# Moving SiLUs, moments and additions between steps, and one product from POOL to VectorE, in a Mamba and mixture-of-experts kernel

## The reference

```python
h = layernorm(layernorm(x)) @ in_proj_w.T            # 256 -> 512 channels
h = silu(sum(pad(h)[k:k + L] * conv_w[:, k] for k in range(4)))
proj = h @ x_proj_w.T                                # dt (1), B (16), C (16)
dt = softplus(proj[0] * dt_proj_w + dt_proj_b)
# for each t, each of 512 channels, each of 16 states n:
state = exp(A[n] * dt[t]) * state + B[t, n] * h[t]
y[t] = sum_n state[n] * C[t, n] + D * h[t]
out = silu(y) @ out_proj_w.T + shortcut
x1 = x + layernorm(out)
# then: x1 + layernorm(shared_swiglu(xn) + routed_swiglu(xn)), 8 experts, the best one per token
```

## Time and profile before

| | |
|---|---|
| median of 3 runs | 1410.12 us |
| the profiled execution | 1411.66 us |
| its span, first to last instruction | 1409.9 us |
| PE busy | 1173.1 us (83%) |
| VectorE busy | 1090.0 us (77%) |
| POOL busy | 1088.5 us (77%) |
| ACT busy | 770.8 us (55%) |
| mean granted TensorE clock | 0.938 of full speed |

### The profile page before, as it was taken

How to read it: one execution, slowest core, us unless ns; L and a number is a source line. 1 busy time by engine, 2 the same in 40 slices (tenths; PEclk the granted TensorE clock), 3 DMA queues, 4 the chain that set the end, 5 groups by cost and what they waited for, 6 DMA issues and landing times.

```text
span 1409.9 us, 15087 instructions
## 1 busy us (share of the span) xinstructions
PE 1173.1 (83%) x4782; PEld 520.5 (37%) x4783; DVE 1090.0 (77%) x1449; ACT 770.8 (55%) x1275; POOL 1088.5 (77%) x565
## 2 busy tenths in 40 slices
PE   5667678786787887888679698788999999999996
PEld 2222223222331422322233242233556655566653
DVE  4598999999999999999998989799241115776675
ACT  5757468676876876867787686556431111111111
POOL 0589999999999999999999999999112824444553
PEclk9898899899999999989998999899999999999998
DMA  3921211240150122124024012300269522222220
GB/s 108 275 67 62 90 60 32 75 150 0 67 189 1 62 99 96 32 75 149 2 74 166 1 62 95 129 0 31 90 237 321 161 75 82 81 81 79 83 66 15
DMA packets 72066, 127.64 MB, mean 91 GB/s; under 512 B 8759, under 2 KB 48448, under 8 KB 67904
## 3 DMA queue, kind: packets, MB, share of 16 engines
q1 hardware_dynamic: 60432, 103.72, 22.2%
q0 software_dynamic: 7152, 16.81, 3.8%
q10 hardware_dynamic: 4416, 6.29, 1.4%
HBM read 97.79 MB, written 31.76 MB: 92 GB/s over the span
## 4 chain that ended last, share of the span: by engine, by line
PE 48%; DVE 21%; ACT 13%; POOL 11%; issue 6%; DMA 0%; DVEq 0%; POOLq 0%; ACTq 0%; SPq 0%
DVE state L1090 12%; PE psX L1647 10%; POOL state L511 6%; PE psX L1582 5%; PE psY L1529 5%; PE bank L1451 4%; PE bank L1486 3%; ACT psX L763 3%; PE psY L1595 3%; POOL bx L500 3%; DVE acc L1025 3%; DVE bx L1078 3%; PE bank L1664 2%; PE psY L1664 2%; POOL lt L516 2%
## 5 line engine op out<-in xcount | busy, mean ns | idle before, releaser
L511 POOL TENSOR_TENSOR state<-state,cbc 128x1024 f32<-128x1024 f32 x256 | 605.8, 2390 | 14.8 <-DVE state L1090 14.7
L1090 DVE TENSOR_TENSOR_SCAN state<-psX,bx 128x1024 f32<-128x1024 f32 x256 | 578.5, 2279 | 31.7 <-ACT psX L763 13.5
L763 ACT ACTIVATE psX<-dt,aneg 128x511 f32<-128x511 f32 x512 | 330.6, 679 | 193.5 <-DVE state L1090 192.8
L500 POOL TENSOR_TENSOR bx<-xh,bbc 128x1024 f32<-128x1024 f32 x120 | 290.3, 2420 | 59.2 <-DMA bbc<-bc_rows 43.3
L1529 PE MATMUL psY<-state,ident 64*64 64x512 f32 x2048 | 284.4, 649 | 18.3 <-POOL state L511 18.3
L1486 PE MATMUL bank<-prow,ident 128*128 128x512 f32 x272 | 170.6, 713 | 114.9 <-DVE bx L1078 114.9
L1078 DVE TENSOR_TENSOR bx<-xh,bank 128x1024 f32<-128x1024 f32 x136 | 162.8, 1197 | 9.3 <-PE bank L1486 9.1
L1529 PEld LDWEIGHTS psY<-state,ident 64*64 64x64 f32 x2048 | 63.9, 139 | 201.7 <-issue 128.8
L961 ACT ACTIVATE sg<-psX 128x512 f32<-128x512 f32 x39 | 23.3, 597 | 196.6 <-PE psX L1647 191.3
L1486 PEld LDWEIGHTS bank<-prow,ident 128*128 128x128 f32 x272 | 48.3, 210 | 205.9 <-DVE bx L1078 169.0
L581 POOL DMA_INDIRECT ysl<-shared_rows,idx x39 | 40.3, 1033 | 80.3 <-DVE idx L1258 75.6
(11 more groups left out here) (200 smaller groups left out, 1726.5 us busy)
## 6 DMA issues: line engine op xcount, KB each, us to landing
cbc<-bc_rows SPq DMA_DIRECT2D x32, 1024.0 KB, 4.7
bbc<-bc_rows SPq DMA_DIRECT2D x16, 1024.0 KB, 6.2
slot_in<-ao SPq DMA_DIRECT2D x1, 5011.5 KB, 35.1
xsl<-slot_in SPq DMA_DIRECT2D x39, 128.5 KB
xin<-in_x SPq DMA_DIRECT2D x8, 512.0 KB, 4.3
xr<-in_x SPq DMA_DIRECT2D x8, 512.0 KB, 5.5
x_rows<-ao SPq DMA_DIRECT2D x8, 512.0 KB, 2.9
xn_rows<-xr SPq DMA_DIRECT2D x8, 512.0 KB, 3.2
```

Of the source, the lines that this page charges most:

```text
L500: nc.gpsimd.tensor_tensor(bx[q % RB][:], xh[par][:, h * CH:(h + 1) * CH], bbc[:, n // 2].unsqueeze(1).broadcast_to([P, CH, L]), ALU.mult). ...
L511: nc.gpsimd.tensor_tensor(w[:], w[:], cbc[:, n].unsqueeze(1).broadcast_to([P, CH, L]), ALU.mult).then_inc(weighted, 1)
L763: e = nc.scalar.activation(decay[q % RD][:, c, 1:L], dt[par][:, h * CH + c, 1:L], ACT.Exp, scale=aneg[:, h * CH + c, n:n + 1])
L1090: nc.vector.tensor_tensor_scan(st[q % RS][:].rearrange("p c t -> p (c t)"), decay[q % RD].rearrange("p c t -> p (c t)"), bx[q % RB][:].rea ...
```

## The change

It does these things:
- step 12 leaves the list of POOL, so VectorE makes 18 products per sequence and POOL 14;
- both SiLUs and the table load behind them are issued at q = 9 instead of 10, so ahead of the decays of step 12;
- the moments of `lead` are computed at q = 24 instead of 29;
- at q = 26 and 27 ACT does the part of `back` ahead of the part of `front`;
- VectorE adds the output projection at q = 17 and 19 instead of 16 and 18, and copies the router's logits at q = 21 instead of 20; TensorE computes those at 20 instead of 19.

```diff
--- before.py
+++ after.py
@@ -37,7 +37,7 @@
     CH = C // H
     Q = H * N
     PN = N // 2
-    BY_POOL = [q % 2 == 0 and q not in (22,) for q in range(Q)]
+    BY_POOL = [q % 2 == 0 and q not in (12, 22) for q in range(Q)]
     PQ = sum(BY_POOL)
     DQ = Q - PQ
     NTH_P = [sum(BY_POOL[:q]) for q in range(Q + 1)]
@@ -633,7 +633,7 @@
                 return last
 
             def lead(f, par, q):
-                if q == 29:
+                if q == 24:
                     act.wait_ge(mv0_ready, f + 1)
                     moments(3, f, mv0[par], 1.0 + EPS, eps2c)
                 if q == 30:
@@ -653,7 +653,7 @@
                     act.wait_ge(inproj_ready, C * f + c + 1)
                     nc.scalar.activation(acc[:, c], psF[:], ACT.Identity,
                                          scale=cw[:, c, TAPS - 1:TAPS]).then_inc(tap_done, 1)
-                if q == 10:
+                if q == 9:
                     act.wait_ge(conv_done, C * (f + 1))
                     if not (isinstance(f, int) and f < 2):
                         act.wait_ge(y_kept, H * (f - 1))
@@ -775,13 +775,15 @@
                         keep_y(i - 1, 1)
                     if do_scan and q == N + SUM_LAG - 1:
                         keep_y(i, 0)
+                    if do_back and q in (26, 27):
+                        back(i - 1, q)
                     if do_front:
                         front(i + 1, 1 - par, q)
-                    if do_back:
+                    if do_back and q not in (26, 27):
                         back(i - 1, q)
                     if not do_front:
                         early(q)
-                    if q == 10 and (do_front or do_back):
+                    if q == 9 and (do_front or do_back):
                         ln_exp_tables()
                     if do_scan and q == 8:
                         act.wait_ge(mv0_ready, i + 1)
...
@@ -1040,13 +1042,13 @@
             def back(b, q):
-                if q in (16, 18):
+                if q in (17, 19):
                     h = q // 2 - 8
...
-                if q == 18:
+                if q == 19:
                     dve.wait_ge(ao_done, 2 * b + 2)
                     stats(1, cb, b, ao, mv[1], mv_ready[1])
...
-                    if do_choose and q == 20:
+                    if do_choose and q == 21:
                         choose(i - 2)
...
@@ -1559,7 +1561,7 @@
-                    if q == 19 and i >= 2:
+                    if q == 20 and i >= 2:
                         choose(i - 2)
```

More of the change, by code:

```diff
@@ L927, in load_group @@
                               xnT_d[LATE_FROM + g]).then_inc(xg_loaded[g % 2], 16)
-            for q in range(10):
+            for q in range(9):
                 back(NB - 1, q)
             keep_y(NB - 1, 1)
-            back(NB - 1, 10)
+            back(NB - 1, 9)
             for c in range(FC):
@@ L1170, in _ @@
             sh_act(0, 0, 1)
-            back(NB - 1, 16)
+            back(NB - 1, 17)
             sh_act(0, 0, 2)
-            back(NB - 1, 18)
+            back(NB - 1, 19)
             sh_act(0, 0, 3)
```

## The result

The changed kernel took 1434.1 us (median; 1431.3 to 1440.1) against 1410.8 for the kernel before on the same chip: ratio 1.0169, interval 1.0154 to 1.0185. Forecast were 1403 and a range that ended at 1415. The profiled execution took 1433.3, its span is 1431.5.

What follows compares the result with a forecast made beforehand. It took a ring of waits through VectorE, ACT and TensorE as the bound, not POOL. Turns 1 to 5 -3.5, turn 6 +0.8, turn 7 +1.1, turn 0 -5.5: -7.1 us, from 1410.12 to 1403.0; range 1390 to 1415.

Steps and rivals of the forecast that it cites:

- Choose moves with 0.12 us: nothing: Router's logits, copied by VectorE a step later: 0.12 us of work changes place, counted as no cost.
- Product 12, the dt projection's delay: On TensorE, spread 13 waits for product 12 and holds the dt projection, which ends at 579.9 against 577.1.
- rival 2: Delayed dt projection runs at half clock on TensorE: +2.6 us in seven turns, +18, giving 1421; chance 0.17.
- The waits that follow: After the dt projection: product 17 starts 1.0 late, scan 17 waits 1.45 more, the addition's 2.18 wait goes.
- the wait of 0.74: VectorE's wait at scan 13, forecast to go because the SiLUs are issued a step sooner.
- The joins: VectorE's two joins wait for a boundary between POOL's instructions: 1.85 and 1.7 us, today 1.35 and 1.77.
- ACT's moves: Moments at step 24, back first in steps 26 and 27: -1.5 us a turn, bounds 0 to -2.5.
- Turn 0: First join starts mid POOL instruction, ends near 144.4 instead of 149.5: -5.1, and -0.4 from the moments, -5.5.
- The end: Turns 6 and 7: +0.8 us without moments to move, +1.1 without a convolution.
- Rival 1: POOL bounds the turn after all, so each turn loses its product, 2.3 us, giving 1391; chance 0.15.
- Rival 3: A join starting in the last 0.2 us before POOL's boundary costs up to 6.9 us: up to 1440; chance 0.06.
- Rival 4: The first turn keeps its long join, as the dt delay there is 2.5 us: only -2, 1408; chance 0.12.

Runs made afterwards that it cites:

- the extra matmuls: The change without the logits' move, plus three matmuls on TensorE in step 9 whose result nothing reads: 1410.9 us, 0.9998 of the kernel before.

## Why the prediction was wrong

- **The step that failed:** "Choose moves with 0.12 us: nothing". I priced the copy on VectorE and not what it waits for. Taking that one line back is worth 18.3 us of the 31 that the forecast missed (by itself, on the kernel before, the move costs 7.2). TensorE's half of the move goes past a spread that waits for VectorE's product, and VectorE's copy follows one step behind: 3.21 us of waiting. VectorE is also later by it, so the join comes without a wait, 0.16 behind the start of a POOL instruction.
- **Product 12, the dt projection's delay:** mechanism right, size short. I let the second spread and its sum run at full clock (to 579.9, last tap + 16.4). In the changed kernel the projection ends at 709.26, last tap + 18.3, since both ran at 1.2 GHz. That is rival 2, priced at 2.6 a turn in seven turns and measured at 2.0 in five. It had 0.17 of the chances. Against it stood that TensorE would be busy in between as before; it was (3.57 of 4.00), and the clock was 0.50 all the same. Giving product 12 back takes 20.8 off the changed kernel, part of it again in the copy's waits (9.5 in place of 18.0), so this and the 18.3 can't be added. The turn that the prediction names, 116.9, is the one that the variant without the logits' move shows when the clock is full.
- **The waits that follow:** right in place and nearly in size. Forecast for product 17 and scan 17 were 1.0 and 1.45 to 1.65, measured 0.85 and 1.59; the wait of 2.18 is gone. Forecast as gone was the wait of 0.74; in its stead product 15 waits 1.90, for the clock.
- **The joins:** forecast 1.85 and 1.7, measured 3.29 and 1.88. I had kept their place against POOL as the square sets it. Late, the join started 0.16 after a POOL instruction and waited for its end. That is so in turns 3 to 5 (3.10 to 3.29); in the other turns the first join takes 1.25 to 1.96.
- **ACT's moves:** forecast -1.5, measured -2.34 in this turn, in company, and alone -1.4 a turn and -5.5 us in all. Right.
- **Turn 0:** right in the number (the join takes 1.34, the turn is 4.3 shorter, forecast 5.5), but by luck. The prediction had the join start in the middle of a POOL instruction. It started at 142.02, after a wait for the square and 0.23 ahead of POOL's next instruction (142.25): POOL is later by the same 0.8, and this is the place at which it was lost before (0.20 ahead, 8.25). This time it won.
- **The end:** forecast +0.8 and +1.1 for turns 6 and 7, measured +7.1 behind turn 5. The copy's waits of 2.22 and 3.06 are there, so this is the first step once more.
- **Rival 1** (POOL the bound) is false for the changed kernel, with POOL idle 9.5 a turn; at 115.4, once the joins are free, it comes near: POOL idles 1.16, and taking product 24 from it gave 0.7 a turn. **Rival 3** (a join loses the port) did not strike the changed kernel but its neighbours, at the price given (6.9): in three of the variants in every second turn. I gave it 0.06, and argued that turns repeat to 0.1 us; those of the kernel before run from 116.10 to 117.95. It came most where several parts that shorten the turn stood together, and took their gain. **Rival 4** did not come about, but the margin that it doubted was gone, as said of turn 0.
- On the Trainium skill (SBUF — State Buffer, section "two separate sides"), that whoever starts first holds the shared ports for its instruction: the 3.29 of a join that started 0.16 after POOL's instruction (2.2 left of it, 1.1 of work) agrees. The lost joins of 8.24 to 8.27, which wait over three instructions though they began ahead of the first, do not.

What stays open: among all first joins that waited for the square and started 0.14 to 0.24 before POOL's next product (67 in the first fourteen traces), 15 were lost and 52 won, with the same lead. Why it is every second turn in two kernels and one turn in seven in another, the traces do not tell. Nor do they tell why TensorE's clock has risen by the second spread in some turns and not in others, with the same idle time and the same work before it, nor why the extra matmuls hold it up in only every second turn.

## What to carry to other kernels

Price both ends of a moved hand-over: a copy that costs 0.2 us waits for whatever its producer is now queued behind, and for that engine's clock. When two changes gain alone and lose together, look in the later one's trace for an instruction that takes several times its usual duration. Here it was one on VectorE with both inputs in SBUF, beside a POOL that did not pause. Then try to make the other engine wait: a pause of 1.2 us freed 7. And look where a hit came from: turn 0 came out as forecast at the very place where it had been lost before.

## What was not expected of the hardware

- A VectorE instruction of 1.1 us on two SBUF inputs took 8.24 to 8.27 us in 15 cases, and 8.36 to 10.77 in four more, always until POOL's first pause, though it had started before POOL's next instruction. Three more, which started 0.37 to 0.70 behind the start of a POOL instruction, took 5.40, 7.46 and 7.47, also until the pause; nine that started 0.16 to 0.34 behind one took 3.10 to 3.29, until its end. With POOL made to wait it never did (28 of 28 first joins in four kernels at 1.22 to 1.36).
- After 5.70 us of idle TensorE ran the next four groups (spread, sum, spread, sum) at 1.2 GHz in some turns (2.08, 1.99, 2.08, 1.99), and had risen by the third in others (2.08, 1.63, 1.12, 1.09): 2 us a turn from that alone.
- The matmuls of the router's logits took 1.95 us at 2.4 GHz and 3.58 at 1.2 GHz.
